# A segment scan with memory: local products in eight tiles of two banks, projection with the tokens held, segment softmax on ScalarE with accumulated sums

## The reference

```python
def step(carry, inp):
    mem, z = carry
    q_s, k_s, v_s, qn_s, kn_s = inp          # qn, kn: before rope
    scores = jnp.einsum('bhnd,bhmd->bhnm', q_s, k_s) * SCALE
    scores = jnp.where(mask, scores, -jnp.inf)
    sdpa = jnp.einsum('bhnm,bhmd->bhnd', jax.nn.softmax(scores, axis=-1), v_s)
    sq = elu1(qn_s)
    num = jnp.einsum('bhnk,bhkv->bhnv', sq, mem)
    den = jnp.einsum('bhnk,bhk->bhn', sq, z)[..., None]
    out = beta * num / (den + 1e-06) + (1.0 - beta) * sdpa
    sk = elu1(kn_s)
    prev_v = jnp.einsum('bhnk,bhkv->bhnv', sk, mem) / jnp.einsum('bhnk,bhk->bhn', sk, z)[..., None]
    mem = mem + jnp.einsum('bhnk,bhnv->bhkv', sk, v_s - prev_v)
    z = z + sk.sum(axis=2)
    return (mem, z), out
```

## Time and profile before

| what | us |
|---|---|
| median of the runs | 3138.38 |
| span of the profiled execution | 3131.4 |
| DVE / ACT / POOL / PE busy over the span | 2510.0 / 1876.0 / 1754.7 / 2658.5 |
| first to last score maximum in the scan | 1371.4 |

### The profile page before, as it was taken

One profiled execution on the slowest core, in us unless ns is written; L12 is line 12 of the kernel. 1 busy time (PEld: TensorE's weight loads), 2 busy tenths in 40 slices (PEclk: granted clock), 3 DMA queues, 4 the chain that ended last, 5 costly groups with the idle time before them and its releaser, 6 DMA issues. The chain is left out here.

```text
span 3131.4 us, 129400 instructions
## 1 busy us (share of the span) xinstructions
PE 2658.5 (85%) x53553; PEld 1508.1 (48%) x53553; DVE 2510.0 (80%) x7597; ACT 1876.0 (60%) x3797; POOL 1754.7 (56%) x1984
## 2 busy tenths in 40 slices
PE   5884999999999999973340899999999999999998
PEld 2441333333333333363230566666666666666665
DVE  4676899999998999766706788888888888888886
ACT  5783899999999999821000455455555555555553
POOL 5871222222222222341063788888888888888886
PEclk9895999999999999986565999999999999999999
DMA  4676344333333343094023000000000000000000
GB/s 135 235 261 178 73 106 94 93 93 99 93 90 96 94 106 94 27 276 122 0 43 89 10 12 11 8 8 11 11 11 11 11 11 11 11 11 5 11 8 11
DMA packets 179263, 209.94 MB, mean 67 GB/s; under 512 B 28592, under 2 KB 140144, under 8 KB 178416
## 3 DMA queue, kind: packets, MB, share of 16 engines
q1 hardware_dynamic: 176112, 200.25, 23.1%
q0 software_dynamic: 2560, 1.35, 0.4%
HBM read 125.10 MB, written 75.63 MB: 64 GB/s over the span
## 5 line engine op out<-in xcount | busy, mean ns | idle before, releaser
L829 ACT ACTIVATE at_pA<-at_ps 128x512 f32<-128x512 f32 x1024 | 551.9, 614 | 83.8 <-DVE at_ps L882 77.1
L891 DVE CUSTOM_DVE_ANT_0 at_junk<-at_ps,w_cmask 128x512 f32<-128x512 f32 (+3 forms) x1024 | 463.4, 485 | 104.4 <-PE at_ps L732 97.1
L882 DVE TENSOR_TENSOR at_ps<-at_ps,w_ratio 128x128 f32<-128x128 f32 (+3 forms) x1024 | 451.2, 491 | 4.7 <-PE at_ps L726 3.1
L701 POOL TENSOR_SCALAR_AFFINE_SELECT at_pB<-at_pB 128x128 f32<-128x128 f32 x256 | 75.4, 294 | 639.6 <-ACT at_pB L835 637.5
L835 ACT ACTIVATE at_pB<-at_ps 128x512 f32<-128x512 f32 (+1 forms) x768 | 379.4, 531 | 53.0 <-PE at_ps L739 47.7
L1980 POOL TENSOR_TENSOR sc_rb<-sc_rb,v_sin 128x512 f32<-128x512 f32 x256 | 326.6, 1276 | 37.6 <-DVE sc_ra L2220 36.2
L2016 PE MATMUL sc_ps<-sc_xT,v_wqkv 128*128 128x512 f32 x512 | 286.1, 641 | 3.9 <-PEq L56 1.4
L726 PE MATMUL at_ps<-at_aq,at_ak 72*128 72x512 bf16 x1024 | 278.3, 388 | 2.7 <-DMA at_ak<-parts_scratch 2.4
L2179 ACT COPY sc_skN<-sc_ps 128x512 f32<-128x512 f32 x128 | 75.1, 587 | 323.6 <-PE sc_ps L2068 323.6
L1975 POOL TENSOR_TENSOR sc_sk<-sc_ee,sc_relu 128x512 f32<-128x512 f32 x128 | 167.0, 1304 | 180.5 <-ACT sc_ee L2170 180.3
L739 PE MATMUL at_ps<-at_bq,at_bk 75*128 75x512 bf16 (+3 forms) x1024 | 265.7, 302 | 1.5 <-ACT at_pB L835 0.9
(11 more groups left out here) (316 smaller groups left out, 5937.4 us busy)
## 6 DMA issues: line engine op xcount, KB each, us to landing
parts_scratch<-fr_parts SPq DMA_DIRECT2D x64, 384.0 KB, 4.1
at_bq<-parts_scratch SPq DMA_DIRECT2D x192, 96.0 KB
at_bk<-parts_scratch SPq DMA_DIRECT2D x192, 96.0 KB
at_aq<-parts_scratch SPq DMA_DIRECT2D x192, 96.0 KB
at_ak<-parts_scratch SPq DMA_DIRECT2D x192, 96.0 KB
v_scratch<-fr_v SPq DMA_DIRECT2D x32, 352.0 KB, 4.3
at_v<-v_scratch SPq DMA_DIRECT2D x32, 352.0 KB, 3.6
parts_scratch<-fr_parts SPq DMA_DIRECT2D x32, 256.0 KB, 3.9
```

The costliest lines, as they stand in the source:

```text
L829: act.activation(pA[:, n % A_RING, j * S:(j + 1) * S], src, ACT.Exp).then_inc(exped, 1)
L882: dve.tensor_tensor(src[:, 0:wide], src[:, 0:wide], W["ratio"][:, S - wide:S], ALU.mult).then_inc(tilted, 1)
L891: ins = dve.tensor_tensor_reduce(junk[:, P * j * (j + 1) // 2:P * (j + 1) * (j + 2) // 2], src[:, col:col + wide], W["cmask"][:, S - wide: ...
```

## The change

Local products: the output partitions of odd groups g are swapped between neighbours (f becomes f^1) and go to bank 7, those of even groups to bank 6, with the head as outer loop. So eight of the array's 32x32 tiles are used, where it was four. Recall by queries and the quantised product's inputs and outputs are swapped alike, and a second copy of x for the residual is loaded in swapped rows (`load_hb`).

Output projection: all eight pairs' turned outputs of a segment are kept, and the projection runs with the turned outputs as the stationary operand, in eight halves (a group of 128 tokens and four pairs each), one half a step from ten steps behind; DVE adds each half to the output (`ydone`). The turning back of the output and its copy go. The program becomes five steps longer.

Softmax: queries' rope tables and mask are negated, so that DVE takes a minimum. ACT computes exp(min - score) out of PSUM, in eight instructions of 32 columns with a bias pointer and an accumulated sum each. DVE takes the reciprocal, POOL multiplies the probabilities by it, DVE transposes them. ACT scales the local products out of PSUM. The addition of the memory's share moves from POOL to DVE, one step later. PE's update waits for the exponentials (`se`) where it waited for the subtraction.

```diff
+def load_hb(sp, seg, j):
+    for f in range(B1):
+        for odd in range(2):
+            to = 32 * swapped(odd, f)
+            sp.dma_start(hb[to:to + 32, j % 2, odd::2], h_seg[f, bass.ds(seg, 1)].rearrange("o i g d -> (o i) g d")[:, odd::2]).then_inc(G[f"hb_in{j % 2}"], 16)
...
 def add_bias(pool, j):
-    wait_h(pool, j)
-    pool.tensor_tensor(hb[:, j % 2], ht[:, j % 2], V["bias"][:].unsqueeze(1).broadcast_to([P, BG, D]), ALU.add).then_inc(G["hb_d"], 1)
+    wait(pool, f"hb_in{j % 2}", 128 * max(1, (j + 1) // 2))
+    pool.tensor_tensor(hb[:, j % 2], hb[:, j % 2], V["bias"][:].unsqueeze(1).broadcast_to([P, BG, D]), ALU.add).then_inc(G["hb_d"], 1)
...
 PT = PER * PAIRS
-STEPS = PT + 5
+HALVES, AFTER = 2 * BG, PAIRS + 2
+STEPS = PT + AFTER
...
+out_half = lambda s: (divmod((s - AFTER) % HALVES, 2), (s - AFTER) // HALVES) if inside(s - AFTER) else None
...
+            load_hb(sp, seg + 1, 1)
             for j in range(PER):
-                wait(sp, "ydone", j + 1)
-                for f in range(B1):
...
                 if j + 3 in readied:
                     wait(sp, "xnn_d", j + 1)
-                    wait(sp, "hb_d", j + 1)
                     load(sp, seg + j + 3, j + 3)
+                if j + 2 in readied:
+                    wait(sp, "ffn_c", j + 1)
+                    load_hb(sp, seg + j + 2, j + 2)
+                wait(sp, "ydone", HALVES * (j + 1))
+                for f in range(B1):
+                    for odd in range(2):
+                        at = 32 * swapped(odd, f)
...
+                p = s - 1
+                if inside(p):
+                    wait(pool, "smd", p + 1)
+                    probs = ss[:, p % 2].rearrange("p (g h) j -> p g h j", h=2)
+                    pool.tensor_tensor(probs, probs, bc(by_ch(sm[:, p % 4]), SEG), ALU.mult).then_inc(G["nrm"], 1)
...
                 for j in at_step(s, 3):
-                    wait(pool, "ffn_c", j - 1)
                     add_bias(pool, j)
-                p = s - 2
-                if inside(p):
-                    wait(pool, "qd", p + 1)
-                    wait(pool, "old", p + 1)
-                    o = ol[:, p % 4].rearrange("p g h d -> p (g h d)")
-                    pool.tensor_tensor(o, o, t2[:, p % 2].rearrange("p c d -> p (c d)"), ALU.add).then_inc(G["od"], 1)
...
-                            ins = pe.matmul(ps[32 * f:32 * f + 32, 2 + hh, g * VE:(g + 1) * VE],
+                            to = 32 * (swapped(g, f) if which == 0 else f)
+                            ins = pe.matmul(ps[to:to + 32, 2 + hh, g * VE:(g + 1) * VE],
...
             def local(p):
-                for g in range(BG):
-                    for hh in range(2):
+                for hh in range(2):
+                    for g in range(BG):
                         for f in range(B1):
-                            ch = 2 * g + hh
-                            ins = pe.matmul(ps[32 * f:32 * f + 32, 6, ch * DH:(ch + 1) * DH], pT[32 * f:32 * f + 32, p % 4, ch, :],
+                            ch, to, col = 2 * g + hh, 32 * swapped(g, f), (2 * (g // 2) + hh) * DH
+                            ins = pe.matmul(ps[to:to + 32, 6 + g % 2, col:col + DH], pT[32 * f:32 * f + 32, p % 4, ch, :],
                                             uu[32 * f:32 * f + 32, p % PAIRS, g, hh, 0:DH], start=True, stop=True)
                 ins.then_inc(G["pvd"], 1)
...
-            def project_out(p):
-                wait(pe, "otc", p + 1)
-                wait(pe, "yt_c", p // PAIRS)
...
-                pe.matmul(ps[:, 7, :], V["wout"][:, h], oT[:, p % 2], start=(h == 0), stop=(h == PAIRS - 1)).then_inc(G["oproj"], 1)
...
-            def turn_y(bank, j):
...
-                    ins = pe.transpose(ps[:, bank, g * P:(g + 1) * P], yT[:, g * P:(g + 1) * P], V["ident"][:])
...
+            def project_out(j, g, half):
+                few = range(half * PAIRS // 2, (half + 1) * PAIRS // 2)
+                for h in few:
+                    ins = pe.matmul(ps[:, 7, YCOL:YCOL + D], oT[:, j % 2, h, g * P:(g + 1) * P], V["wout"][:, h], start=(h == few[0]), stop=(h == few[-1]))
+                ins.then_inc(G["oproj"], 1)
...
                     wait(pe, "otc", min(s - 3, PT))
+                    wait(pe, "ydone", s - AFTER)
                     wait(pe, "pt", p + 1)
                     local(p)
...
-                p = s - 4
-                if inside(p):
-                    project_out(p)
+                if out_half(s):
+                    (g, half), j = out_half(s)
+                    wait(pe, "old", min(s - 1, PT))
+                    wait(pe, "otc", j * PAIRS + 4 * half + 4)
+                    wait(pe, "ydone", s - AFTER)
+                    project_out(j, g, half)
...
-                    wait(pe, "sx", min(s, PT))
+                    wait(pe, "se", min(s, PT))
...
+                p = s - 2
+                if inside(p):
+                    wait(act, "pvd", p + 1)
+                    wait(act, "ott", p - 3)
+                    local = ps[:, 6:8, 0:256].rearrange("p b (q h d) -> p b q h d", h=2, d=DH)
+                    to = ol[:, p % 4].rearrange("p (q b) h d -> p b q h d", b=2)
+                    for hh in range(2):
+                        col = 2 * (p % PAIRS) + hh
+                        ins = act.activation(to[:, :, :, hh], local[:, :, :, hh], ACT.Identity, scale=V["rest"][:, col:col + 1])
+                    ins.then_inc(G["old"], 1)
...
                     wait(act, "sx", p + 1)
-                    act.activation(ss[:, p % 2], ss[:, p % 2], ACT.Exp).then_inc(G["se"], 1)
+                    wait(act, "nrm", p - 1)
+                    wait(act, "pt", p - 1)
+                    for ch in range(GH):
+                        g, hh = divmod(ch, 2)
+                        n = hh * BG + g
+                        ins = act.activation(ss[:, p % 2, ch], ps[:, 4 + hh, g * SEG:(g + 1) * SEG], ACT.Exp, bias=mx[:, n:n + 1], scale=-1.0,
+                                             accum_out=sm[:, p % 4, n:n + 1])
+                    ins.then_inc(G["se"], 1)
...
-                p = s - 4
-                if inside(p) and p % PAIRS == PAIRS - 1:
-                    wait(act, "oproj", p + 1)
-                    wait(act, "yt", p // PAIRS)
-                    act.copy(yT[:], ps[:, 7, :]).then_inc(G["yt_c"], 1)
...
                     wait(act, "ott", p + 1)
-                    wait(act, "oproj", p - 1)
-                    act.copy(oT[:, p % 2], ps[:, 6, :]).then_inc(G["otc"], 1)
+                    if p // PAIRS >= 2 and p % PAIRS == 0:
+                        wait(act, "oproj", HALVES * (p // PAIRS - 1))
+                    act.copy(oT[:, p // PAIRS % 2, p % PAIRS], ps[:, 6, :]).then_inc(G["otc"], 1)
...
-                p = s - 2
-                if inside(p):
-                    wait(dve, "pvd", p + 1)
-                    wait(dve, "pt", p + 1)
...
-                    local = ps[:, 6, :].rearrange("p (g h d) -> p g h d", h=2, d=DH)
-                    for hh in range(2):
-                        col = 2 * (p % PAIRS) + hh
-                        ins = dve.scalar_tensor_tensor(ol[:, p % 4, :, hh], local[:, :, hh], V["rest"][:, col:col + 1],
-                                                       bc(head(sm[:, p % 4])[:, hh], DH), ALU.mult, ALU.mult)
-                    ins.then_inc(G["old"], 1)
...
-                    link(dve.tensor_reduce(head(mx[:]), scored, AX.X, ALU.max))
-                    dve.tensor_tensor(by_head(ss[:, p % 2]), scored, bc(head(mx[:]), SEG), ALU.subtract).then_inc(G["sx"], 1)
+                    wait(dve, "se", p)
+                    dve.tensor_reduce(head(mx[:]), scored, AX.X, ALU.min).then_inc(G["sx"], 1)
...
+                p = s - 3
+                if inside(p):
+                    wait(dve, "old", p + 1)
+                    wait(dve, "qd", p + 1)
+                    o = ol[:, p % 4].rearrange("p g h d -> p (g h d)")
+                    dve.tensor_tensor(o, o, t2[:, p % 2].rearrange("p c d -> p (c d)"), ALU.add).then_inc(G["od"], 1)
...
+                p = s - 1
+                if inside(p):
+                    wait(dve, "se", p + 1)
+                    dve.reciprocal(sm[:, p % 4], sm[:, p % 4]).then_inc(G["smd"], 1)
                 if s < PT:
                     rope(2 * s + 1)
                 p = s - 1
                 if inside(p):
-                    wait(dve, "se", p + 1)
-                    dve.transpose(pT[:, p % 4].rearrange("p c j -> p (c j)"), ss[:, p % 2].rearrange("p c j -> p (c j)"))
-                    s_ = sm[:, p % 4]
-                    link(dve.tensor_reduce(head(s_), by_head(ss[:, p % 2]), AX.X, ALU.add))
-                    dve.reciprocal(s_, s_).then_inc(G["pt"], 1)
+                    wait(dve, "nrm", p + 1)
+                    dve.transpose(pT[:, p % 4].rearrange("p c j -> p (c j)"), ss[:, p % 2].rearrange("p c j -> p (c j)")).then_inc(G["pt"], 1)
...
-                if s - 12 in starts:
-                    j = (s - 12) // PAIRS
-                    wait(dve, "yt", j + 1)
```

(14 more changed lines are left out.)

28 lines of the change are left out of this document (10 added, 18 removed).

## The result

The changed kernel takes 3505.1 us (median; 3498.7 to 3513.2) against 3140.3 us for the kernel before on the same chip (3136.6 to 3144.0): a ratio of 1.116, 95% interval 1.114 to 1.118. Its profiled execution has a span of 3511.2 us for the 3131.4 of before.

What follows compares the result with a forecast made beforehand. The loop through the softmax binds: 9.07 us from scores to local products, 4.12 behind, 0.09 quantised addition, 0.9 clock: 14.2 a step for 10.8. Over 127 steps +432, tail +6, on 3138.4: 3576 us, range 3350 to 3700.

Steps and rivals of the forecast that it cites:

- 1, T0 to the exponentials: From T0, the end of a step's scores, through DVE's minimum and hand-overs to ACT's exponentials: 0.50 us.
- 2, eight exponentials with reads: On ACT, eight exponentials of 32 columns at 0.22 us plus 0.14 for each accumulator read: 3.0 us, bounds 1.9 and 3.9.
- 3, to the feature map on POOL: From the end of the exponentials, through ACT's features of the next keys, to POOL's start on the feature map: 1.71 us.
- 4, POOL's queue and normalisation: On POOL, feature map 1.23 and value correction 1.15 ahead of the normalisation's own 0.64: 3.02 us.
- 5, transpose, addition, hand-over: On DVE, transpose 0.44, addition of the projected half 0.29 and hand-overs, ahead of the local products: 0.84 us.
- local products to T0, clock aside: On PE, start of the local products to the end of the next scores: 4.40 less 0.28 for eight tiles, 4.12 us.
- clock: PE at half clock behind long gaps: about 1.4 us on the loop, charged at 5/8, +0.9 us a step, bounds 0 and 1.4.
- Rival (a): The same loop with PE's clock held at 2.4 GHz: 13.28 us a step, 3459 us; chance 25%.
- The tail: Behind the last turned heads, 4.8 us before; then seven halves follow one another at 1.54 us: +6 us.
- Rival (c): Local products on eight tiles run no faster than on four: 14.5 us a step, 3611 us; chance 14%, on top of either.
- Rival (d): PE's work binds, not the loop, if local products start under 5.3 us behind the scores: 9.8 a step, 3017 us; 4%.
- None of these three engines' sums sets the pace; their order does, so I count these at nothing: Work added to and taken off DVE, POOL and ACT, the moved addition included, was charged 0 us as engine sums.

Runs made afterwards that it cites:

- the filled kernel: The changed kernel with eight more unused products of 128 columns in PE's gap ahead of the local products: 3405.6 us, ratio 1.088.
- the repaired kernels: The changed kernel with POOL's normalisation ahead of its feature map: 3190.1 us; with the rotation of the next keys also ahead of the value correction: 3189.2 us.
- the first experiment: The changed kernel with POOL's normalisation of the probabilities moved ahead of the feature map and value correction: 3190.1 us, ratio 1.017.

## Why the prediction was right, and where its terms were off

The forecast was 3576 us, with 3350 to 3700 around it; 3505 came. The mechanism was the one named: the loop through the softmax, lengthened by ACT and by POOL's queue, with a gap on PE and a low clock behind it. Moving one instruction of POOL's left 57 of the 365 us lost, which shows it.

| term | forecast | measured |
|---|---|---|
| 1, T0 to the exponentials | 0.50 | 0.50 (2409.71 to 2410.21) |
| 2, eight exponentials with reads | 3.0 | 2.26 (2410.21 to 2412.47) |
| 3, to the feature map on POOL | 1.71 | 1.71 (2412.47 to 2414.18) |
| 4, POOL's queue and normalisation | 3.02 | 3.02 (2414.18 to 2417.20) |
| 5, transpose, addition, hand-over | 0.84 | 0.72 (2417.20 to 2417.92) |
| T0 to local products | 9.07 | 8.21; mean 8.24 |
| local products to T0, clock aside | 4.12 | 4.53 (gap filled) |
| clock | 0.9 | 0.86 (5.39 - 4.53) |
| step | 14.2 | 13.66 |

**Term 2 was mis-sized,** by what the read adds to each exponential, the part that was guessed. An exponential is 0.297 us in mean (0.32 worked out), and the read exists as an instruction of its own, at 0.216 us, the upper bound. But it overlaps on both sides: 0.18 us from exponential to read, 0.10 from read to the next exponential, 0.26 to 0.28 for the pair where 0.22 + 0.14 was taken. The forecast let exponentials overlap one another and set the read on top without any; the start-to-start time of the pair is the unit, not the length of its parts.

**PE behind the local products was too short.** The earlier trace rows is a step without a gap. The mean step of before has 4.96 us there, not 4.40, and 5.85 to the local products, not 6.17. Two single steps thus gave 10.57 where the mean is 10.81: 0.32 too much ahead of the local products, 0.56 too little behind them, and a forecast of the kernel before by the same sum would have come out 0.23 us a step too short. Runs of PE are now and then broken by about 1 us that the profile puts down to "issue": 41 times by over 0.7 us between the first and the last maximum of before, 0.29 us a step in mean, as in this row, a piece of the scores. In the filled kernel such breaks behind the local products make 0.13 us a step, so they are a part of the difference only:

```profile
2294.82 0.26 PE L2061 MATMUL sc_ps<-sc_kr,sc_qr 64*32 64x32 f32 x7 [1.05 <-issue]
```

What lies between 14.18 (forecast) and 13.63 (8.24 + 5.39) is then: term 2 -0.74, PE +0.41, term 5 -0.12, the extra work of single steps ahead of the local products -0.06 (8.24 - 8.21 for the 0.09 charged), the clock -0.04.

**The clock** cost what was charged, 0.81 by the filled gap and 0.86 by the local products to T0 alone (5.39 - 4.53). Rival (a), the clock held, gave 3459 at 13.28 us a step; the filled kernel, which is that rival made real, came to 3406 at 12.85, lower by the same errors in the other terms.

**The tail** grew by 11 us, not 6. The halves that come last follow one another every 1.60 us, for the 1.54 forecast; among the steps that run out ahead of them there is one at the low clock. Line 2099 in the last part of the timeline:

```profile
3486.23 2.07 PE L2099 MATMUL sc_ps<-v_wout,sc_oT 128*128 128x128 f32 x8
...
3498.14 1.13 PE L2099 MATMUL sc_ps<-v_wout,sc_oT 128*128 128x128 f32 x8 [0.59 <-DVE sc_y L2324]
3499.74 1.13 PE L2099 MATMUL sc_ps<-v_wout,sc_oT 128*128 128x128 f32 x8 [0.47 <-DVE sc_y L2324]
```

**Rival (c)** is out. Local products that send four row tiles into each of two banks take 0.79 us from start to start (2405.92 to 2406.71 in the filled kernel), the 0.79 forecast, for 1.07 before. The rule of the Trainium skill's page "TensorEngine Tiling (Array Packing)", section "Restrictions and Gotchas", that different row tiles can't use one bank at the same time, isn't seen in the time here; in this kernel the tiles of a bank write different partitions of it.

**Rival (d)** said that PE's work decides, at 3017 us, if POOL normalises first. With that order made real the kernel took 3190. Local products under 5.3 us behind T0, the point from which it decides, were never reached: they stood at 6.21, held in 46 steps by ACT's copy of the turned heads, of which the forecast didn't speak.

```profile
PEld sc_ps L2070 <- ACT sc_oT L2226: 52.9, 46, 3.1
```

**"None of these three engines' sums sets the pace; their order does, so I count these at nothing"** is the step of the forecast that failed without harm. The first half held. From it follows that a moved instruction has to be priced by its place, and the moved addition, counted at nothing, costs 1.1% alone.

What the repaired kernels lose against before, 0.3 to 0.4 us a step, is told in part only. The local products start 0.36 us later (6.21 for 5.85), most of which the exponentials alone show (6.20 when they alone are added; by the scores' own end it is 6.23 for 5.96); the addition alone costs as much and the two don't add. The 0.28 us that eight tiles save is not seen in the sum: local to T0 is 4.95, as before. In the first experiment the rotated keys came at 9.68 us and held the masks in 49 steps, for 2 before; with the keys earlier, local to T0 fell by no more than 0.06. PE's idle time between the local products and the minimum tells most of it: 0.51 us a step in the first experiment, 0.17 of it for those keys, against 0.30 before, so 0.22 of the 0.28 saved is idled away. With the keys earlier it is still 0.50, nearly all of it put down to "issue", and what that is stays open. So does whether the copy of the turned heads, moved ahead of the features, would make the change pay; that wasn't tried.

## What to carry to other kernels

Work taken off a busy engine is worth nothing where a loop of waits sets the pace; add up what stands *in front of* each new instruction in its engine's queue, since the normalisation of 0.63 us cost 2.5 us a step by its place, the clock's share in it. When the loop lengthens, ask what the bound engine does in its new gap: here idleness cost another 0.8 us a step through the clock. And take the split of a loop from means over many steps, not from one clean step.

## What the runs showed of the hardware

**Accumulated sums on ScalarE.** Each exponential of 32 columns with `accum_out` is followed by an ACTIVATION_READ_ACCUMULATOR. The two groups of the changed kernel (busy us, mean ns):

```profile
L2216 ACT ACTIVATE sc_ss<-sc_ps,sc_mx 128x32 f32<-128x32 f32 x1024 | 277.5, 297 | 36.2 <-DVE sc_mx L2281 36.2
...
L2216 ACT ACTIVATION_READ_ACCUMULATOR sc_ss<-sc_ps,sc_mx 128x1 f32 x1024 | 221.5, 216 | 0.0
```

Both overlap their neighbours, and a pair costs 0.26 to 0.28 us. Eight pairs of 32 columns take 2.26 us where one exponential of 256 takes 0.42: the split by columns is dear.

**The clock.** In the changed kernel PE stood idle before the local products of nearly every step, and in the stretch behind the gap shown above the granted clock was 0.58:

```profile
2417.90:2422.00 4.10, 4.08 (x137) 3.54 (x137) 2.96 (x6) 0.84 (x2) 3.34 (x4) 0.58 0.02 4
```

The values in it ran at 1.2 GHz (2.08 us), the recall behind them partly (1.19 for 0.86), the turned keys at 2.4 GHz again (0.66). Over the scan an instruction of the values takes 0.406 us in mean for the 0.291 of before.

**One addition, two lengths.** The addition of 128x512 with both inputs in SBUF, on DVE, in two steps of the first experiment, with POOL's rows beside the first (at the second POOL was idle from 2314.66 to 2318.69):

```profile
2302.62 1.26 POOL L2004 TENSOR_TENSOR sc_qr<-sc_ra,sc_rb 128x512 f32<-128x512 f32 x1
2302.76 1.67 DVE L2293 TENSOR_TENSOR sc_ol<-sc_ol,sc_t 128x512 f32<-128x512 f32 x1
...
2316.78 0.68 DVE L2293 TENSOR_TENSOR sc_ol<-sc_ol,sc_t 128x512 f32<-128x512 f32 x1
```

The first ended 0.55 us after POOL did (2304.43 against 2303.88), as if it had done most of its work only then. Of its 128 instances there, 73 took longer than 0.7 us, 1.33 in mean: every one began while an instruction of POOL's was running, and every one ended 0.545 to 0.553 us behind that instruction's end. The other 55 took 0.68; 38 of them began with POOL idle, and 16 of the other 17 when POOL's instruction had 0.04 to 0.10 us left. It goes the other way too: 13 of POOL's additions of line 2004 began while DVE's was running, and took 1.67 to 1.69 us for 1.27; the one that began 0.01 us ahead of DVE's took 1.83. So these rows look as if the two never did their work at the same time and one waited out the whole of the other. The multiplications of lines 2275 and 2301, of the same size but with one input in PSUM, take 0.69 whether POOL works at their start (145 of them) or not (111). The Trainium skill's page "GPSIMD Engine Reference", section "8. Key points", names contention with VectorE for instructions with two SBUF inputs; these rows agree with it. So the addition costs more on DVE than its 0.68 us: in the kernel before with that addition alone moved, it took 0.92 us in mean.
